# Moving the per-chunk builds of a gated delta-rule kernel from VectorE to GpSimd, and reordering its weight preparation

## The reference

```python
q, k, v, gate = x @ Wq.T, x @ Wk.T, x @ Wv.T, x @ Wg.T     # 16 heads of 64
beta  = sigmoid(x @ Wb.T)
alpha = exp(-exp(A_log) * softplus(x @ Wa.T + dt_bias))     # one per head
q = q / norm(q) / sqrt(64);  k = k / norm(k)
def step(S, k_t, q_t, v_t, beta_t, a_t):                    # 2048 steps
    S = S * a_t
    delta = (v_t - k_t @ S) * beta_t
    S = S + outer(k_t, delta)
    return S, q_t @ S
ctx = rmsnorm(ys) * silu(gate)
x = x + layernorm(ctx @ Wo.T + bo)
# linear: inputs and weights to FP6 (E2M3) in blocks of 32, scaled by the block's maximum
x = x + layernorm(dequant(quant(layernorm(x))) @ dequant(quant(Wf)).T + bias)
```

## Time and profile before

| | us |
|---|---|
| median of 3 runs | 7010.18 (7008.75 to 7017.97) |
| the profiled execution | 7021.37 |
| its span, slowest core (7) | 7019.8 |
| spans of the other cores | 6984.7 to 7015.0 |
| TensorE busy | 2711.2 (39%) |
| VectorE busy | 2782.2 (40%) |
| ScalarE busy | 1049.1 (15%) |
| GpSimd busy | 677.5 (10%) |

### The profile page before, as it was taken

One profiled execution on the slowest core, in us unless ns is written; L12 is line 12 of the kernel. 1 busy time (PEld: TensorE's weight loads), 2 busy tenths in 40 slices (PEclk: granted clock), 3 DMA queues, 4 the chain that ended last, 5 costly groups with the idle time before them and its releaser, 6 DMA issues.

```text
span 7019.8 us, 73180 instructions; the slowest of 8 cores (6984.7 to 7019.8 us)
## 1 busy us (share of the span) xinstructions
PE 2711.2 (39%) x22136; PEld 1586.7 (23%) x22136; DVE 2782.2 (40%) x6462; ACT 1049.1 (15%) x2243; POOL 677.5 (10%) x1048
## 2 busy tenths in 40 slices
PE   3204234444414434444422515444431515444441
PEld 1101122322301112323311203223220103223220
DVE  1350134444462124444454114444445014444446
ACT  1111111111111111111111211111111211111111
POOL 1100111101000111111000011011000011011000
PEclk9999555555556655555556755555555855555555
DMA  5412021212102112112101112112111212121210
GB/s 91 70 27 66 11 43 31 46 30 42 35 12 65 31 31 38 39 30 44 44 14 48 46 20 48 32 34 43 40 26 36 58 14 46 30 38 39 44 32 21
DMA packets 426947, 269.76 MB, mean 38 GB/s; under 512 B 235380, under 2 KB 413942, under 8 KB 426566
## 3 DMA queue, kind: packets, MB, share of 16 engines
q1 hardware_dynamic: 382790, 212.59, 13.8%
q0 software_dynamic: 43776, 52.49, 4.8%
HBM read 245.93 MB, written 27.44 MB: 39 GB/s over the span
## 4 chain that ended last, share of the span: by engine, by line
DVE 32%; DMA 27%; PE 18%; issue 14%; ACT 6%; DVEq 2%; POOL 0%; SPq 0%; ACTq 0%; POOLq 0%
DMA wrep<-wd 14%; DVE ptm L817 8%; DVE u L821 7%; PE ppr L490 3%; DVE rr L564 3%; PE ptr L826 2%; PE psu L839 2%; DMA wdst<-sc 2%; DVEq L1123 2%; DVE rr L878 1%; PE pys L852 1%; PE ptr L556 1%; DVE st L428 1%; ACT ut L831 1%; DMA prow<-pd 1%
## 5 line engine op out<-in xcount | busy, mean ns | idle before, releaser
L826 PE MATMUL ptr<-idf,u 128*16 128x128 f32 x1024 | 259.1, 407 | 1454.2 <-DVE u L821 1350.5
L743 DVE TENSOR_TENSOR wrep<-wrep,bb 128x2048 f32<-128x2048 f32 x128 | 293.4, 2292 | 1086.1 <-DMA wrep<-wd 1086.1
L817 DVE TENSOR_TENSOR ptm<-wrep,u 128x120 f32<-128x120 f32 (+14 forms) x1920 | 515.6, 269 | 195.0 <-DVE u L821 8.4
L821 DVE TENSOR_TENSOR u<-u,ptm 128x120 f32<-128x120 f32 (+14 forms) x1920 | 452.8, 236 | 212.6 <-DVE ptm L817 16.7
L775 PE MATMUL pkv<-kc,s 64*64 64x16 f32 x4096 | 479.7, 265 | 45.2 <-DVE kc L751 45.2
L775 PEld LDWEIGHTS pkv<-kc,s 64*64 64x64 f32 x4096 | 454.4, 220 | 74.1 <-issue 69.9
L780 PE MATMUL pys<-qc,s 64*64 64x16 f32 x4096 | 460.6, 264 | 21.3 <-ACT ys L859 21.3
L826 PEld LDWEIGHTS ptr<-idf,u 128*16 128x16 f32 x1024 | 100.4, 112 | 1600.9 <-issue 1561.2
L780 PEld LDWEIGHTS pys<-qc,s 64*64 64x64 f32 x4096 | 450.7, 222 | 30.1 <-issue 30.1
L490 PE MATMUL ppr<-lt,wrhs 128*128 128x512 bf16 x1280 | 345.2, 418 | 213.3 <-DMA wrhs<-wtk 30.6
L845 DVE TENSOR_TENSOR s<-s,psu 128x512 f32<-128x512 f32 x128 | 88.1, 688 | 752.7 <-PE psu L839 752.7
(11 more groups left out here) (193 smaller groups left out, 4103.7 us busy)
## 6 DMA issues: line engine op xcount, KB each, us to landing
wrep<-wd SPq DMA_DIRECT2D x256, 512.0 KB, 5.3
sx<-x SPq DMA_DIRECT2D x4, 2048.0 KB, 8.0
ao<-pd SPq DMA_DIRECT2D x32, 256.0 KB, 5.0
out<-sx SPq DMA_DIRECT2D x4, 2048.0 KB, 6.6
wld<-Wf SPq DMA_DIRECT2D x8, 512.0 KB, 3.5
wrhs<-wtq POOLq DMA_DIRECT2D x16, 256.0 KB, 3.7
wrhs<-wtq SPq DMA_DIRECT2D x16, 256.0 KB, 3.1
wrhs<-wtk SPq DMA_DIRECT2D x16, 256.0 KB, 3.0
```

What stands on the lines that cost most here:

```text
L743: VE(lambda e, wv=wv, bb3=bb3: e.tensor_tensor(wv, wv, bb3, ALU.mult), [f"wrep{cp}", "bb"], [f"wrep{cp}"], tag="wrepscale")
L817: VE(lambda e, wsl=wsl, ub=ub, ptv=ptv: e.tensor_tensor(ptv, wsl, ub, ALU.mult), ["u", f"wrep{cp}"], ["ptm"], tag="slv_p")
L821: VE(lambda e, usl=usl, ptv=ptv: e.tensor_tensor(usl, usl, ptv, ALU.add), ["u", "ptm"], ["u"], tag="slv_u")
L826: TE(lambda e, hp=hp, hpi=hpi: e.transpose(p_tr[0:16, hpi * 128:(hpi + 1) * 128], s_u[:, hp * C:(hp + 1) * C], s_idf[:]), ["u", "idf", "ptr"],
```

## The change

It has three parts. The three builds of `chunk_builds` are recorded for GpSimd in place of VectorE, with the same operands and names, at the same place. The function `proj_superblock` is cut in two, and the first half (load, layer norm and transposes of x) is run for superblock 0 ahead of the weight stage, the second half behind it. And the blocks of Wo and Wf alternate: a block of Wo is loaded into `xd`, transposed through `ptp` with all copies on ScalarE into `tb`, and stored, then a block of Wf is prepared as before. The transposes of the weights use other PSUM banks.

```diff
+    def prep_weight_alt_iter(d_src, d_dst, ob):
+        for hb in range(2):
+            dma("gpsimd", s_xd[:, hb * 512:(hb + 1) * 512],
+                d_src[ob * 128:(ob + 1) * 128, hb * 512:(hb + 1) * 512],
+                [], ["xd" + "AB"[hb]], tag="wload")
+        for fb in range(8):
+            slot = fb % 4
+            hk = "xd" + "AB"[fb // 4]
+            wk = "tb" + "AB"[fb // 4]
+            TE(lambda e, fb=fb, slot=slot: e.transpose(
+                p_tp[:, slot * 128:(slot + 1) * 128],
+                s_xd[:, fb * 128:(fb + 1) * 128], s_idb[:]),
+               [hk, "idb", "ptp"], ["ptpw"])
+            SE(lambda e, fb=fb, slot=slot: e.copy(
+                s_tb[:, fb * 128:(fb + 1) * 128],
+                p_tp[:, slot * 128:(slot + 1) * 128]),
+               ["ptpw"], ["ptp", wk])
...
+    def emit_preamble():
+        proj_x_part(0)
+        for m in "qkvgb":
+            prep_weight(d_w[m], d_wt[m], tagn=m)
+        for ob in range(8):
+            prep_weight_alt_iter(d_wo, d_wto, ob)
+            prep_weight_quant_iter(d_wf, d_wtf, ob)
...
+        proj_mm_part(0)
...
-        VE(lambda e: e.tensor_tensor(s_kc[:].rearrange("p (h t) -> p h t", h=NP),
+        GE(lambda e: e.tensor_tensor(s_kc[:].rearrange("p (h t) -> p h t", h=NP),
                                      kbsl, e1sl, ALU.mult),
            ["kb", "e1"], ["kc"])
-        VE(lambda e: e.tensor_tensor(s_qc[:].rearrange("p (h t) -> p h t", h=NP),
+        GE(lambda e: e.tensor_tensor(s_qc[:].rearrange("p (h t) -> p h t", h=NP),
                                      qbsl, e1sl, ALU.mult),
            ["qb", "e1"], ["qc"])
-        VE(lambda e: e.tensor_tensor(s_k2[:].rearrange("p (h t) -> p h t", h=NP),
+        GE(lambda e: e.tensor_tensor(s_k2[:].rearrange("p (h t) -> p h t", h=NP),
                                      kbsl, e2sl, ALU.mult),
            ["kb", "e2"], ["k2"])
...
+    emit_preamble()
     for sb in range(NSB):
-        proj_superblock(sb)
+        if sb > 0:
+            proj_superblock(sb)
```

More of the change, by code:

```diff
@@ L382, in prep_weight @@
             for fb in range(8):
-                bank, bkey = (p_pr, "ppr") if fb % 2 == 0 else (p_sc, "psc")
+                if quantize:
+                    bank, bkey = (p_kv, "pkv") if fb % 2 == 0 else (p_sc2, "psc2")
+                else:
+                    bank, bkey = (p_pr, "ppr") if fb % 2 == 0 else (p_kv, "pkv")
                 hk = "wbf" + "AB"[fb // 4]
@@ L404, in prep_weight @@
                 dma("sync", dst, src, ["wtt" + "AB"[hb]], [], tag="wstore")
[L406 to L421, removed]
@@ L422, in build_program @@
-    dma("sync", d_wat.rearrange("(fb f) h -> f fb h", f=128),
-        s_wtt[:, 0:128].rearrange("f (fb h) -> f fb h", h=16), ["wttA"], ["wttA"])
+    def prep_weight_alt_iter(d_src, d_dst, ob):
[15 more added lines that the diff above has]
+               ["ptpw"], ["ptp", wk])
+        for hb in range(2):
+            dst = d_dst.rearrange("(fb f) o -> f fb o", f=128)[
+                :, hb * 4:(hb + 1) * 4, ob * 128:(ob + 1) * 128]
+            srcs = s_tb[:, hb * 512:(hb + 1) * 512].rearrange(
+                "f (fb o) -> f fb o", o=128)
+            dma("sync", dst, srcs, ["tb" + "AB"[hb]], [], tag="wstore")
@@ new lines, in prep_weight_quant_iter @@
+    def prep_weight_quant_iter(d_src, d_dst, ob):
+        dma("sync", s_wld[:], d_src[ob * 128:(ob + 1) * 128, :],
+            [], ["wld"], tag="wload")
+        emit_quantize(s_wld[:], s_wbf[:], "wld", ["wbfA", "wbfB"])
+        for fb in range(8):
+            bank, bkey = (p_kv, "pkv") if fb % 2 == 0 else (p_sc2, "psc2")
+            hk = "wbf" + "AB"[fb // 4]
+            wk = "wtt" + "AB"[fb // 4]
+            TE(lambda e, fb=fb, bank=bank: e.matmul(
+                bank[:, 0:128],
+                s_wbf[:, fb * 128:(fb + 1) * 128], s_idb[:],
+                start=True, stop=True),
+               [hk, "idb", bkey], [bkey + "w"])
+            if fb % 2 == 0:
+                SE(lambda e, fb=fb, bank=bank: e.copy(
+                    s_wtt[:, fb * 128:(fb + 1) * 128], bank[:, 0:128]),
+                   [bkey + "w"], [bkey, wk])
+            else:
+                VE(lambda e, fb=fb, bank=bank: e.tensor_copy(
+                    s_wtt[:, fb * 128:(fb + 1) * 128], bank[:, 0:128]),
+                   [bkey + "w"], [bkey, wk])
+        for hb in range(2):
+            dst = d_dst.rearrange("(fb f) o -> f fb o", f=128)[
+                :, hb * 4:(hb + 1) * 4, ob * 128:(ob + 1) * 128]
+            srcs = s_wtt[:, hb * 512:(hb + 1) * 512].rearrange(
+                "f (fb o) -> f fb o", o=128)
+            dma("sync", dst, srcs, ["wtt" + "AB"[hb]], [], tag="wstore")
@@ new lines, in emit_preamble @@
+    def emit_preamble():
[5 more added lines that the diff above has]
+            prep_weight_quant_iter(d_wf, d_wtf, ob)
+        dma("sync", s_wld[0:16, :], d_wa, [], ["wld"])
+        VE(lambda e: e.tensor_copy(s_wbf[0:16, :], s_wld[0:16, :]), ["wld"],
+           ["wbfA", "wbfB"])
+        for fb in range(8):
+            slot = fb % 4
+            TE(lambda e, fb=fb, slot=slot: e.transpose(
+                p_tp[:, slot * 128:slot * 128 + 16],
+                s_wbf[0:16, fb * 128:(fb + 1) * 128], s_idb[0:16, 0:16]),
+               ["wbfA", "wbfB", "idb", "ptp"], ["ptpw"])
+            SE(lambda e, fb=fb, slot=slot: e.copy(
+                s_wtt[:, fb * 16:(fb + 1) * 16], p_tp[:, slot * 128:slot * 128 + 16]),
+               ["ptpw"], ["ptp", "wttA"])
+        dma("sync", d_wat.rearrange("(fb f) h -> f fb h", f=128),
+            s_wtt[:, 0:128].rearrange("f (fb h) -> f fb h", h=16), ["wttA"], ["wttA"])
+        proj_mm_part(0)
@@ L444, in ln_stats, with proj_x_part @@
         VE(lambda e: e.reciprocal(s_st[:, 1:2], s_st[:, 1:2]), ["st"], ["st"])
-    def proj_superblock(sb):
+    def proj_x_part(sb):
         xsrc = d_x.rearrange("(n p) d -> p n d", p=128)[:, sb * 4:(sb + 1) * 4, :]
@@ L474, in proj_superblock, with proj_mm_part @@
                        [bkey + "w"], [bkey, "lt"])
+    def proj_mm_part(sb):
         projs = [("q", s_qb, AF.Identity), ("k", s_kb, AF.Identity),
@@ L686, in scores_and_masks, with proj_superblock @@
             piece()
+    def proj_superblock(sb):
+        proj_x_part(sb)
+        proj_mm_part(sb)
     def ebuild_window(sb, wi):
```

## The result

The changed kernel takes 7389.26 us (median of 8 runs, 7384.56 to 7396.91) against 7010.32 us before: a ratio of 1.054, 95% interval 1.0529 to 1.0552. It is 379 us slower. Direction and place were as forecast, the size was not: 275 us were forecast, and 7389 lies above the range of 7180 to 7350. The profiled execution has a span of 7387.1 us, 367.3 more than before.

A forecast was written before the change was run, and what follows sets the result against it. No engine was full; a chain of waits, largest for `wrep`, bounded the kernel. Profiled 7021.4 + 263 (late triples) + 8 (on-time builds) + 5 (weight stage) = 7297, in median terms 7286; forecast 7285 us, own range 7235 to 7345, wider 7180 to 7350.

The forecast's parts named there:

- Triples stand behind the DMA chains: Chunks 3, 4 and 7 of twelve windows: builds on GpSimd wait for the piece's last DMA issue, 263 us in all.
- The price of a late triple: Last DMA issue 0.56 us, `kc` and `qc` 1.15, TensorE's 32 products 3.6: 5.3 us until `pkv` is ready.
- To be compared with the start of L802: Lateness is last issue plus 5.3 us against the present start of L802, VectorE's `u` minus `pkv`.
- Chunk 3 late by 11.5 us in the first window: Triple 3 stands behind 16 DMAs; products end at 1040.7 against L802's start at 1029.19.
- Chunk 4 "takes the place of the 11.5 and is not added to it": Triple 4 stands behind mask work and 8 dumps; first window 13.0 us late in all, replacing chunk 3's delay.
- Chunk 7, another 8.7 us in the first window: Triple 7 stands behind 8 extracts, mask work and 8 dumps; its delay adds, giving 21.7 us for the first window.
- VectorE is spared 0.55 us, sharing costs 0.7: On-time builds, 52 times: -29 us spared, +37 us from GpSimd contending with VectorE's scale and solve; +8 us together.
- Weight stage +5 us: First `wtq` load exposed +3 us, Wo blocks between Wf blocks +2; range -44 (Wo hidden wholly) to +20.
- Rival E: GpSimd's DMA waits sit in its queue, so builds pass them and no triple is late: 6950 to 7010 us; chance 0.05.
- B: Weight stage: Wo is hidden wholly behind VectorE's quantising of Wf, giving 7236 us; chance 0.07.
- rival D: GpSimd's DMA chain shortens as waiting VectorE keeps `wrep` loads away, 5 us from each of 24 stalls: 7165; chance 0.11.
- C: Builds on GpSimd are as dear as its wide form, 1.93 us each, with upper-end contention: 7395 us; chance 0.07.

The follow-up runs named there:

- experiment 6: Changed kernel with a separate name for each of the eight row groups that GpSimd's DMAs write, so they stop waiting for one another: 6729.7 us.
- experiment 4: Changed kernel with the triples for chunks 3, 4 and 7 of the twelve windows with pieces built on VectorE: 6986.84 us, ratio 0.9964.
- experiment 1: Changed kernel with the three builds back on VectorE, leaving the new weight stage and early normalisation: 7018.45 us, ratio 1.001.
- 2: Kernel before with only the three builds moved to GpSimd, weight stage as before: 7385.95 us, ratio 1.0541.
- experiment 3: Changed kernel with the readers of `e1` taken out of what a reused DMA slot waits for: 7343.78 us, ratio 1.0475.
- experiment 5: experiment 3 with piece 3, holding the mask's exponential, recorded ahead of the products of chunk 3: 7301.01 us, ratio 1.0408.
- experiment 7: Kernel before, builds on VectorE, with separate names for the row groups that GpSimd's small DMAs write: 6765.57 us, ratio 0.9648.
- experiment 9: Kernel before with builds on GpSimd, separate names for the small DMAs and for each half of a `wrep` load: 6647.33 us, ratio 0.948.

## Why the prediction was wrong, point by point

- *Triples stand behind the DMA chains, and that makes it slower.* Right: 36 late waits, none once the chains are gone (experiment 6) or the late triples are back on VectorE (4), and all of the loss from the builds (1, 2).
- *The price of a late triple, 5.3 us from the last issue to the products' end.* Nearly right. It is 1043.20 less 1042.63, two builds, and the products to 1048.0: 5.4 us. GpSimd's builds take 0.43 to 0.44 us, inside the forecast 0.4 to 0.6.
- *To be compared with the start of L802.* One step short. The decay in front of it waits for the same products, so 0.6 us more, twice in each window, 14 us in all.
- *Chunk 3 late by 11.5 us in the first window.* Right: by the same sum it is 10.4 in the mean of twelve, and chunk 1 to 3 grew by 9.6.
- *Chunk 4 "takes the place of the 11.5 and is not added to it", because the load has moved and "the dumps have not, since they wait for `prow` and not for VectorE".* **This is the step that failed.** By the sum, chunk 4 would be 3.1 us later than chunk 3 in the mean of twelve windows; it was 11.9. Three things had moved between the last `prow` issue and L866 of chunk 4. The first dump is issued 11.3 us after that `prow` and not 7.0, since the mask needs an exponential on ScalarE, whose stream held the copies behind the late products: +4.3. The 8 dumps take 17.8 us and not 22.2, since no load runs beside them: -4.5. And from the last dump to L866 it is 14.9 us and not 5.3, because the `wrep` load for chunk 5 waited for the late triple through the slot rule: +9.6, 0.7 of which chunk 3 has too. In the time, experiment 3 took out 45 us and experiment 5 another 43, together 88 of the 104 us between forecast and result.
- *The remaining 16 us.* No run separates them; they are what is left of terms of both signs. The decay adds 14. The chain for chunk 7 adds some 19 and the shorter first chain takes off 16 (next point). The triples on time were 17 to 30 us cheaper than forecast. And 11 us of the forecast were the distance of one profiled run from the median. That experiment 5 comes so near 7285 is therefore in part luck.
- *Chunk 7, another 8.7 us in the first window.* Too small: by the same sum 8.3 in the mean of twelve, measured 10.3. Besides the decay, the chain from its first extract to its last dump was taken over as it stood, 49.9 us, and takes 51.5 after. The first chain, of 16 DMAs, went from 49.8 to 48.5.
- *VectorE is spared 0.55 us, sharing costs 0.7.* The first holds, the second was mis-sized. It was read from GpSimd's mask operations in the solve, which fall there at the same place after (11.2 to 11.6 us in chunk 3 against 10.3). The builds fall beside the `wrep` scale and the decay. There GpSimd loses most: `kc` has a median of 437 ns and a mean of 730, one beside the scale took 1.35 us, while the scale kept its 2293 ns. But the decay, which is on the path, pays as well, 0.92 us in place of 0.69 in each of 36 chunks with builds beside it (rows in experiment 4). This belongs to the rule of the Trainium skill, "GPSIMD Engine Reference", section Key points, that the two contend where VectorE reads two SBUF inputs. The runs agree that they contend, and show that at the builds' place both lose, GpSimd more. The sum had +8 us for the 52 triples on time; at 0.17 to 0.42 gained for each it should have had -9 to -22.
- *Builds at window starts hidden.* Right: the stretches between windows changed by 3 us in all, though TensorE waits 9.3 us there.
- *Weight stage +5 us.* Right: 3 us at the first projection (591.1 against 588.0), 8 in the time.
- *Rival E, builds that pass the DMA waits.* Excluded: each first build starts within 0.02 us of the end of the last issue. All 36 do. B did not happen (experiment 1). D happened in one place, the dumps ahead of chunk 4, where a load that is held back leaves GpSimd's chain 4.5 us shorter; but it was held by the slot's wait, which cost more. C's 7395 lies 6 us from the result by luck: none of its terms is there, the builds that made TensorE wait late took 0.43 to 0.44 us and not 1.93.

## What to carry to other kernels

Before a short operation goes to an idle engine, read what stands before it in that engine's stream, not how busy the engine is. Then follow the delay one round further: all that waits for the late result holds up its own stream, and an exponential, a slot or a load behind it can be the next delay. And a wait that a planner adds by a name, and which costs nothing while the names' readers are early, becomes real when one of them moves to a late engine; list the waits of the built program before and after. Where such chains come from one name for disjoint parts of a buffer, splitting the name was worth more here (249 us, experiment 7) than any placement. After such a split look at the issues again: a rule that works by names can put the old wait back, as it did for 60 of 128 loads in experiment 9.

## What had not been expected of the hardware

- A `kc` build beside VectorE's 128x2048 product took 1.05 to 2.08 us in 35 chunks, against 0.43 alone, and VectorE's 2.29 us hardly changed (at most 2.38). Beside the 128x512 decay both lost: `qc` took 0.87 us against 0.43, the decay 0.92 against 0.69.
- The slowing of small DMAs beside a `wrep` load was forecast in rival D (up to 5 us against 2.5), but not that holding the load back, by a wait that nobody had meant, gives back 5.0 of the 8.8 us that this wait costs.
- Two 512 KB loads issued 0.6 us apart instead of 5 are both in 8.0 us after the first issue instead of 10.6. An estimate from these rows: the second takes 7.4 us beside the first and 5.5 by itself, so they slow each other, but only by part of what going together gains.
